# Weight splitting moves off GpSimd, and the bookkeeping of the choice moves to PSUM, in a gated attention and expert kernel

## The reference, cut to what matters

```
x = x + tanh(g_xattn) * mix(layernorm(x), softmax(q(ctx) k(ctx)^T))
n = layernorm(x)
logits = gelu(n @ rw1) @ rw2                 # 8 experts
wgt, idx = top_k(softmax(logits), 2)
for e in range(8):
    Ye = gelu(n @ w1[e] + b1[e]) @ w2[e] + b2[e]
    Ce = gelu(b1[e]) @ w2[e] + b2[e]
    for k in range(2):
        out += any(idx[..., k] == e) * wgt[..., k] * where(idx[..., k] == e, Ye, Ce)
x = x + tanh(g_ffn) * out
```

## Time and profile before

| | us |
|---|---|
| median of 3 runs | 200.49 |
| the 3 runs | 199.53 to 202.08 |
| the profiled execution | 201.76 |
| its span | 199.9 |
| busy, PE / DVE / ACT / POOL | 161.8 / 133.5 / 102.4 / 115.6 |
| mean granted TensorE clock | 0.939 of full speed |

### The profile page before, as it was taken

How to read it: one execution, slowest core, us unless ns; L and a number is a source line. 1 busy time by engine, 2 the same in 40 slices (tenths; PEclk the granted TensorE clock), 3 DMA queues, 4 the chain that set the end, 5 groups by cost and what they waited for, 6 DMA issues and landing times.

```text
span 199.9 us, 5212 instructions
## 1 busy us (share of the span) xinstructions
PE 161.8 (81%) x1722; PEld 137.8 (69%) x1723; DVE 133.5 (67%) x294; ACT 102.4 (51%) x256; POOL 115.6 (58%) x173
## 2 busy tenths in 40 slices
PE   6899995948169999599498599699499999998930
PEld 2457983814059999499397599598499999886610
DVE  2666589788635779989996266945566677464185
ACT  0588977727828999469487144243044433440000
POOL 0029999999868999678886414454155444203100
PEclk9999999996967999889999999999999999999955
DMA  6899354598377655945509435556166666430495
GB/s 178 252 387 331 123 152 169 181 279 271 118 211 256 232 175 201 320 147 177 197 21 387 139 113 225 216 228 234 46 241 249 247 232 219 192 113 33 125 325 200
DMA packets 21028, 40.69 MB, mean 204 GB/s; under 512 B 2741, under 2 KB 12047, under 8 KB 21010
## 3 DMA queue, kind: packets, MB, share of 16 engines
q1 hardware_dynamic: 17680, 34.54, 49.6%
q0 software_dynamic: 1872, 4.73, 7.4%
q10 hardware_dynamic: 1458, 1.19, 1.8%
HBM read 23.66 MB, written 4.60 MB: 141 GB/s over the span
## 4 chain that ended last, share of the span: by engine, by line
PE 45%; POOL 17%; DVE 13%; DMA 11%; issue 7%; SPq 3%; DVEq 1%; ACT 1%; POOLq 0%; ACTq 0%
POOL w_lo L401 11%; PE bank L1299 8%; PE bank L1301 7%; PE bank L1300 7%; PE bank L1310 7%; PE bank L1312 7%; PE bank L1311 7%; DMA stage<-in_L_ffn_w 4%; POOL w_hi L408 3%; DMA stage<-y_table 3%; DVE lnT L952 2%; DMA x_table<-probT 2%; DMA probT<-x_table,gidx 2%; DVE en L923 2%; DMA y_table<-lnx,ycol 1%
## 5 line engine op out<-in xcount | busy, mean ns | idle before, releaser
L654 ACT ACTIVATE bank<-bank,b1T 128x128 f32<-128x128 f32 x152 | 42.3, 342 | 57.7 <-PE bank L1301 57.7
L1310 PE MATMUL bank<-w_hi,cf 128*128 (+1 forms) x152 | 41.8, 275 | 9.8 <-DVE lnT L952 9.8
L401 POOL TENSOR_TENSOR w_lo<-stage,w_hi 128x256 bf16<-128x256 f32 x64 | 48.2, 787 | 0.7
L1311 PE MATMUL bank<-w_lo,cf 128*128 (+1 forms) x152 | 41.8, 275 | 0.8 <-issue 0.8
L1312 PE MATMUL bank<-w_hi,lnT 128*128 (+1 forms) x152 | 41.9, 276 | 0.0
L1300 PE MATMUL bank<-cfT,stage 128*128 128x128 bf16 x176 | 34.0, 219 | 0.0
L1299 PE MATMUL bank<-cfT,stage 128*128 128x128 f16 x176 | 34.0, 219 | 0.0
L1301 PE MATMUL bank<-cfT,stage 128*128 128x128 f16 x176 | 34.0, 219 | 0.0
L418 POOL TENSOR_TENSOR held<-cst 128x1 f32<-128x1 f32 x31 | 6.8, 218 | 39.0 <-DVE lnx L965 37.7
L952 DVE TENSOR_TENSOR lnT<-bank,cf 128x512 bf16<-128x512 f32 x38 | 26.1, 688 | 4.0 <-ACT cf L661 3.3
L519 ACT ACTIVATE w_hi<-stage 128x1024 f16<-128x1024 f32 x24 | 25.0, 1049 | 7.1 <-POOL cfT L414 5.6
(11 more groups left out here) (195 smaller groups left out, 340.7 us busy)
## 6 DMA issues: line engine op xcount, KB each, us to landing
stage<-in_L_ffn_w SPq DMA_DIRECT2D x32, 512.0 KB, 4.6
stage<-w_hi SPq DMA_DIRECT2D x12, 512.0 KB, 3.0
stage<-w_lo SPq DMA_DIRECT2D x12, 512.0 KB, 3.7
stage<-y_table SPq DMA_DIRECT2D x8, 256.0 KB, 4.7
xs<-in_x SPq DMA_DIRECT2D x2, 512.0 KB, 7.9
out<-stage SPq DMA_DIRECT2D x4, 256.0 KB, 2.7
cf<-in_ctx SPq DMA_DIRECT2D x1, 512.0 KB, 5.4
x_table<-cfT ACTq DMA_DIRECT2D x2, 256.0 KB, 4.2
```

What stands on the lines that cost most here:

```text
L401: last = nc.gpsimd.tensor_tensor(out=w_lo[:, q, n:n + PIECE], in0=stage[:, q % RING, n:n + PIECE], in1=w_hi[:, q, n:n + PIECE], op=ALU.sub ...
L654: last = nc.scalar.activation(h, h, ACT.Gelu, bias=bias)
L1310: mm(o, h_hi[:, u, c, :], w2_hi[:, ex, 1, c, :], start=(c == 0), stop=False)
L1311: mm(o, h_hi[:, u, c, :], w2_lo[:, ex, 1, c, :], start=False, stop=False)
```

## The change

- ScalarE and VectorE take over quarters that GpSimd split: `POOL_HIGHS` loses 9 and 27, `DVE_QUARTERS` becomes 6, 7 and all from 11 on. GpSimd keeps 0 to 5 whole and the low parts of 8, 9 and 10. Behind the index it issues DMAs only.
- GpSimd does the four `token_low` before the low parts 8 to 10; ScalarE does its `token_high` and `xnT_copy(1)` earlier, and its highs 8 to 11 among the sends.
- ScalarE does highs 12 to 15 ahead of block 0, and 16 to 31 in the 16 halves of the static blocks, one behind each.
- VectorE has new lists `ahead` and `behind`; the bookkeeping steps stand in front of `behind` and write their scratch to PSUM (`aside`, halves of banks 2 and 3, and bank 5) where it was SBUF.
- SyncE waits for the first gather before quarter 16, where it was 17.
- TensorE's register loads move from behind block 7 into it, and there are more `keep_busy` products: 4 and 4 new in the router stage, 12 for 6, 8 for 4, 14 for 9.

```diff
-        DVE_QUARTERS = (6, 7, 11, 12, 13, 15, 17, 19, 20, 22, 23, 26, 28, 29, 30, 31)
-        POOL_HIGHS = (0, 1, 2, 3, 4, 5, 9, 27)
+        DVE_QUARTERS = (6, 7) + tuple(range(11, QUARTERS))
+        POOL_HIGHS = (0, 1, 2, 3, 4, 5)
...
-                if q == 17:
+                if q == 16:
                     sp.wait_ge(gathered[0], 16)
...
             own(0, 6)
-            lows(8, 9)
-            token_low(0)
-            own(9, 10)
-            token_low(1)
-            token_low(2)
-            token_low(3)
-            lows(10, 11)
+            for b in range(4):
+                token_low(b)
+            lows(8, 11)
             wait(index_ready, 1)
...
-            lows(14, 15)
             refill(6, 0, 2, 16)
-            lows(16, 17)
             wait(yidx_ready, 1)
             put(0, 0)
             refill(7, 1, 3, 16)
-            lows(18, 19)
-            put(1, 1)
-            lows(21, 22)
-            put(2, 0)
-            lows(24, 25)
+            for i in range(1, 4):
+                put(i, i % 2)
...
-            high(13, 17)
+            high(12, 16)
...
+            later = [q for q in range(16, QUARTERS) if q not in POOL_HIGHS]
             for i in range(NS):
                 for half in range(2):
                     gelu_half(i, i % 2, i, half)
                     hidden_high(i, i % 2, half)
-                    q = 17 + 2 * i + half
-                    if q >= 27:
-                        q += 1
-                    high(q, min(q + 1, QUARTERS))
+                    if 2 * i + half < len(later):
+                        high(later[2 * i + half], later[2 * i + half] + 1)
...
-                step(nc.vector.tensor_tensor(out=en[:, :], in0=en[:, :], in1=eend, op=ALU.add))
...
-                step(nc.vector.tensor_tensor(out=oh_rest, in0=iota_b[:, N_EXP:BLOCKS].unsqueeze(1).broadcast_to(kb),
+                step(nc.vector.tensor_tensor(out=same, in0=iota_b[:, N_EXP:BLOCKS].unsqueeze(1).broadcast_to(kb),
                                              in1=blk_i.unsqueeze(2).broadcast_to(kb), op=ALU.is_equal))
...
-            low(11)
-            low(12)
-            scatter_rows(0, N_EXP)
+            scatter_rows(0, N_EXP, first, scratch[:, 0:N_EXP])
             counts_of_choices()
             dve.wait_ge(tr_w, 2)
             nc.vector.tensor_copy(b1T[:, :], bank[7][:, 0:HC * N_EXP])
+            low(11)
             xT_copy(0, 0)
+            low(12)
+            xT_copy(1, 1)
             low(13)
-            xT_copy(1, 1)
             hidden_low(0, 0, 0)
-            ahead = {0: (15,), 1: (19,), 2: (20,), 3: (22,), 4: (23,), 5: (26,), 6: (30,)}
-            behind = {0: (17,), 5: (28, 29), 6: (31,)}
+            ahead = {0: (14, 15), 1: (17,), 2: (19, 20), 3: (22,), 4: (24, 25), 5: (27, 28), 6: (30,)}
+            behind = {0: (16,), 1: (18,), 2: (21,), 3: (23,), 4: (26,), 5: (29,), 6: (31,)}
...
             xnT_tr(1)
+            keep_busy(4, 1, filler)
             router_hidden(1)
+            keep_busy(4, 1, filler)
...
+                        if i == NS - 1 and c == 1:
+                            pe.wait_ge(eb_ready, 1)
+                            pe.reg_mov(experts[0], NS - 1)
+                            pe.load(experts[1], eb[0:1, 2 * JS:2 * JS + 1])
+                        elif i == NS - 1 and c == 3:
+                            pe.wait_ge(used_ready, 1)
+                            jl = last_pair(pe)
+                        elif i == NS - 1 and c == 5:
+                            used = used_blocks(pe)
...
-            pe.wait_ge(eb_ready, 1)
-            pe.reg_mov(experts[0], NS - 1)
-            pe.load(experts[1], eb[0:1, 2 * JS:2 * JS + 1])
-            pe.wait_ge(used_ready, 1)
-            jl, used = last_pair(pe), used_blocks(pe)
             wait_weights(pe, QUARTERS - 1)
```

More of the change, by code:

```diff
@@ L474, in _ @@
             refill(7, 1, 3, 16)
-            lows(18, 19)
-            put(1, 1)
-            lows(21, 22)
-            put(2, 0)
-            lows(24, 25)
+            for i in range(1, 4):
+                put(i, i % 2)
             wait(index_ready, 2)
             refill(NS, 0, 4, 32)
-            put(3, 1)
-            lows(25, 26)
-            own(27, 28)
             put(4, 0)
@@ L903, in rest_of_blocks @@
+            def rest_of_blocks(spare):
+                starts = spare[:, 0:N_EXP]
+                rslot, blk_i = [spare[:, TOPK * T * n:TOPK * T * (n + 1)].bitcast(I32) for n in (1, 2)]
+                slotb = spare[:, TE:2 * TE].rearrange("p (t e) -> p t e", t=T)
+                rprod = spare[:, 2 * TE:4 * TE].rearrange("p (k t e) -> p k t e", k=TOPK, t=T)
+                same = bank[5][:, D:D + TOPK * T * REST].rearrange("p (k n) -> p k n", n=REST)
                 rank_te = rank_s[:, :].rearrange("p (t e) -> p t e", t=T)
-                step(nc.vector.tensor_tensor(out=slotb, in0=rank_te, in1=e_bc(st_[:, :]), op=ALU.add))
+                step(nc.vector.tensor_copy(starts, st_[:, :]))
+                step(nc.vector.tensor_tensor(out=slotb, in0=rank_te, in1=e_bc(starts), op=ALU.add))
@@ L917, in rest_of_blocks, with experts_of_blocks @@
                                         in1=tokp1.rearrange("p k t -> p (k t)").unsqueeze(2).broadcast_to(kb),
                                         op=ALU.mult).then_inc(rest_ready, 1)
-            def experts_of_blocks():
-                step(nc.vector.scalar_tensor_tensor(out=en[:, :], in0=more[:, 0:N_EXP], scalar=float(P), in1=st_[:, :],
-                                                    op0=ALU.mult, op1=ALU.add))
-                step(nc.vector.tensor_tensor(out=en[:, :], in0=en[:, :], in1=eend, op=ALU.add))
+            def experts_of_blocks(spare):
+                ends = spare[:, 0:N_EXP]
+                found = spare[:, 2 * N_EXP:2 * N_EXP + BLOCKS]
@@ new lines, in experts_of_blocks @@
+                step(nc.vector.tensor_copy(ends, en[:, :]))
+                step(nc.vector.scalar_tensor_tensor(out=behind_end, in0=iota_b.unsqueeze(2).broadcast_to(be),
+                                                    scalar=float(P), in1=ends.unsqueeze(1).broadcast_to(be),
+                                                    op0=ALU.subtract, op1=ALU.is_ge))
+                step(nc.vector.tensor_reduce(out=found, in_=behind_end, axis=X, op=ALU.add))
+                nc.vector.tensor_scalar(eb[:, :], found, float(N_EXP - 1), None, ALU.min).then_inc(eb_ready, 1)
@@ new lines, in used_counts @@
+            def used_counts(spare):
+                ends = spare[:, 0:N_EXP]
+                used_f = spare[:, N_EXP:N_EXP + 3]
+                whole = spare[:, 2 * N_EXP:2 * N_EXP + 3].bitcast(I32)
+                used = ((0, P + LEAST_LAST * 2 * P, 2 * P), (1, LEAST_ODD * 2 * P, 2 * P), (2, LEAST * P, P))
+                for n, least, size in used:
+                    last = nc.vector.tensor_scalar(used_f[:, n:n + 1], ends[:, N_EXP - 1:N_EXP], float(least - P), None,
+                                                   ALU.subtract)
+                step(last)
+                step(nc.vector.tensor_copy(whole, used_f))
+                for n, least, size in used:
+                    last = nc.vector.tensor_scalar(used_i[:, n:n + 1], whole[:, n:n + 1], size.bit_length() - 1, None,
+                                                   ALU.logical_shift_right)
+                last.then_inc(used_ready, 1)
```

106 lines of the change are left out of this document (43 added, 63 removed).

## The result

| | us |
|---|---|
| before, median of 4 runs | 200.92 (199.53 to 202.08) |
| after, median of 4 runs | **215.18** (213.03 to 216.37) |
| ratio, 95% interval | 1.0677 (1.0543 to 1.0811) |
| after, profiled execution / its span | 213.03 / 210.9 |
| mean granted clock, before / after | 0.939 / 0.935 |

The change is slower by 6.8%, and the forecast of 213.5 holds. The two profiled executions, 201.76 and 213.03, lie 11.3 us apart. All that follows compares spans and places within the profiled executions.

A forecast was written before the change was run, and what follows sets the result against it. GpSimd bounds the kernel ahead of block 0, TensorE from there on. Terms -2.0 - 0.8 - 9.7 + 0.7 + 4.2 + 16.3 + 4.5 = +13.2 on 201.76 give 215.0, stated as a 213.5 us median, range 206 to 219.

The forecast's parts named there:

- start and fillers: Ahead of and in block 0: earlier first gather, -2.0 us, and more dummy products raising block 0's clock, -0.8 us.
- waits of the blocks 1 to 4 that go: TensorE's waits of 2.2 and 2.9 us behind VectorE's stalled steps, and 1.45 us of low clock, disappear: -6.6 us.
- VectorE's excess: VectorE's loop turns 1 to 4 outlast TensorE's 5.5 us, giving waits of about one us at blocks 3 to 6: +4.2.
- four chains of late highs, with their clock: Blocks 6 to 8: TensorE waits on engines taking turns, +16.3 us, and the clock falls between, +4.5 us.
- loads in block 7: TensorE's register loads leave the end of block 7, saving 3.1 us, and cost 0.7 (0 to 3.1) between its columns.
- The late highs: Highs 28 to 31 stand behind gelus of blocks 6 and 7; four chains of 4.84 us, waits of 4.2: +16.3 us.
- "faster" rival: The highs are ready at each VectorE low, so the chain and its clock drop out: 192.9 us, chance 0.05.
- The clock: Blocks 6 to 8: three falls of 1.5 us behind the four idle stretches, +4.5 us (0 to +7.5).
- The start: Ahead of block 0: first gather at 49.6 instead of 52.63 us, 1.0 given back beside VectorE's low(11): -2.0 us.
- A rule on GpSimd's DMAs: First gather: the skill's 3100 ns for a DMA of 620 would put it, and the sum, 1.5 us later.
- What goes: Blocks 2 to 8: PSUM scratch frees two stalled steps, one low clock goes, loads leave block 7's end: -9.7 us.
- The fillers: Dummy products in the router stage, around the choice and ahead of block 0 shorten idle time: -0.8 us (0 to -1.5).

The follow-up runs named there:

- experiment 1: Changed kernel with ScalarE's high parts early again (22 and 23 together, 25 and 26 together), so 28 to 31 stand behind blocks 5 and 6: 195.06 us, ratio 0.9725.
- experiment 2: Kernel before with only the highs of quarters 28 to 31 one block later, behind the gelus of blocks 6 and 7: 214.65 us, ratio 1.0735.
- experiment 9: Changed kernel with the low parts of quarters 16, 21 and 26 back on GpSimd, ScalarE's high parts still late: 213.73 us, ratio 1.0774.
- experiment 4: Kernel before with only TensorE's register loads moved into block 7 (columns 1, 3 and 5): 199.88 us, ratio 1.0003.
- experiment 3: Kernel before with only the bookkeeping functions of the change, scratch of the choice steps in PSUM: 195.75 us, ratio 0.9789.
- experiment 7: Kernel of experiment 1 with the low parts of quarters 16, 21 and 26 given back to GpSimd: 192.48 us, ratio 0.9591.
- experiment 5: Kernel before with only the change's added dummy products (12, 8 and 14, and 4 behind each router transpose): 201.19 us, ratio 0.9965.
- experiment 8: Kernel of experiment 1 with the dummy products as before (6, 4 and 9, none behind the router transposes): 193.35 us, ratio 0.9619.
- experiment 10: Kernel of experiment 7 with the dummy products as before (6, 4, 9 and none behind the router transposes): 193.66 us, ratio 0.9639.
- experiment 11: Kernel of experiment 1 with TensorE's register loads put back behind block 7: 197.71 us, ratio 0.9895.
- experiment 6: Kernel before with only GpSimd's order changed, its four low parts of the tokens ahead of quarters 8 to 10: 201.74 us.
- experiment 12: Kernel before with the change's order ahead of the index on both GpSimd and ScalarE, quarter 9's high part on ScalarE: 199.4 us, ratio 0.9972.

## Why the prediction was right, step by step

The working was against the profiled execution, where it said +13.2 and the two profiled executions show +11.3. (215.0 less 1.27 is 213.7; the forecast said 213.5.) By its own terms, from the `y_copy` times above:

| | forecast | in the trace |
|---|---|---|
| start and fillers | -2.8 | -4.9 |
| waits of the blocks 1 to 4 that go, VectorE's excess | -6.6 + 4.2 = -2.4 | -2.8 |
| four chains of late highs, with their clock | +16.3 + 4.5 = +20.8 | +22 |
| loads in block 7 | -3.1 + 0.7 = -2.4 | -3.1 |

The loads' -3.1 is the 3.09 us that before loses there, and the +22 is what then remains of the 18.8 us between the `y_copy` of blocks 4 and 7. Some of the nearness of the total is chance: the start came out 2.1 us better than forecast and the clock 1.8 worse, which nearly cancels.

- **The late highs** are the step that decided the sign, and it held in its place, its order and its size. The forecast had waits of 4.2 us from a chain of 4.84; measured were 4.07, 3.42, 4.07 and 3.96, and the chain from the first gelu at 92.95 to the product at 97.64 is 4.69, where the forecast, without its first link of 0.19, has 4.65. Block 6 ends 20.0 us later than by before's pace, and of the low clock 1.9 us lie behind that, which makes 22. Experiments 1 and 2 show the cause by taking it out and by putting it in alone (-20.1 and +13.7 us). That it isn't VectorE's load is shown by experiment 2, which has VectorE's old list, and by experiment 9, which takes three low parts from it. The forecast's "faster" rival needed high 28 to be ready when VectorE came to its low part; VectorE waited 2.26 to 6.58 us each time.
- **The clock** was put too low: 6.3 us, where three falls of 1.5 were taken, 4.5 in all. All four pieces ran mostly at the low level, as the upper end of the term (7.5) had it. The pure waits were then a little less than forecast: about 22 - 6.3 = 15.7 against 16.3.
- **The start** was underrated by 2.1 us, if the two profiled executions are taken as they are. But the one of before has a late block 0: in experiments 2 and 4, which have before's start unchanged, `y_copy` of block 0 is at 67.08 and 66.73 instead of 68.64. So 1.6 to 1.9 of the 4.9 can be the execution and not the change, and 3.0 to 3.3 are then left against the forecast's 2.8. GpSimd's working came out nearly to the number: low parts of the tokens done at 41.15 (forecast 41.6), the gather at 48.89 (49.6). What did not come was the microsecond given back for `low(11)` beside the first gather: that gather took 1.12 us with `low(11)` beginning 0.27 us behind it, as long as before, and its data landed after 2.91 us instead of 3.60. TensorE began at 51.85 (forecast 54). One reading of the forecast was wrong: in the chain of before GpSimd's splitting doesn't run without a break up to the first gather. From 45.64 on the chain goes over ScalarE's queue, two high parts and the last transfer of the tokens to the table:

```profile
47.87 3.88 DMA x_table<-probT
```

It landed at 51.75, and GpSimd's last four pieces ended at 52.31. In experiment 3, where those pieces took 3.53 us instead of 4.52, GpSimd waited 1.25 us for the same transfer. So two things came late together in the kernel before, and the four `token_low` at the front of the list move both.
- **A rule on GpSimd's DMAs.** The forecast weighed the 3100 ns against 620 that the Trainium skill, page "SBUF — State Buffer", section "SBUF: two separate sides", gives for a DMA whose descriptors GpSimd can't write beside VectorE. The page gives them for a `tensor_copy` on VectorE; a `low` is a `tensor_tensor`, which by its subsection "Who interferes with whom" did not stall a DMA in the probe described there. So the page spoke less against the change than the forecast had it. The traces lie between the two. Gathers that begin while a `low` is already running are longer than the undisturbed 0.95: 1.83 us at 52.84 beside a `low` from 52.63 to 53.85, and in experiment 1 1.65 at 50.44 beside one up to 51.26, 1.92 at 56.37 beside one up to 57.46, and 1.14 at 53.66 beside one up to 53.98. The lengthening, 0.88, 0.70, 0.97 and 0.19, is each time a little less than what was left of the `low` (1.01, 0.82, 1.09 and 0.32). The first gather, which began ahead of the `low`, paid nothing.
- **What goes.** The two steps that stood still go with the PSUM scratch (experiment 3), and that alone gives 2.1%, 4 to 5 us; the fall of the clock at 83 to 86 us goes with them. The Trainium skill, page "SBUF — State Buffer", section "Who interferes with whom", says that a VectorE instruction with two inputs in SBUF contends with a GpSimd instruction that reads SBUF, and that the port is locked for one of them alone. With one input moved to PSUM the 2.18 us became 0.43 in experiment 3 while GpSimd was splitting, and the trace agrees.
- **VectorE's excess** came as forecast, as waits of about one us: 0.69, 1.10, 1.20 and 0.52 at 73, 77, 87 and 91 us, 3.5 in all for 4.2. In the same stretch experiment 1 waits 4.2 us and experiment 7, with three low parts less on VectorE, 1.9.
- **The loads** cost nothing inside block 7 (5.53 us from transposes to transposes in experiment 4), the lower end of what was allowed (0 to +3.1).
- **The fillers** gave nothing that can be measured (experiments 5 and 8), where -0.8 was taken. In the trace of after the clock was low in block 0 all the same (0.50 from 54 to 56 us).

What stays open: on what it depends whether the clock falls behind a wait of 2.8 us or not. At the same place of the program, in or behind the same wait of 2.8 us, it fell in the traces of experiments 1, 4, 7, 8, 10 and 11, and not in those of before, after and experiments 2, 3, 5, 6, 9 and 12. Each is one execution, so it isn't shown either whether this belongs to the kernel or to the execution. No run here was made to settle that. Nor was the move of the low parts from GpSimd to VectorE tried alone; experiment 7 takes back three of them.

## What to carry to other kernels

When work moves between engines, write down for each consumer the order in which its inputs come out of the producer's list, and look for an item that stands behind something that needs the consumer's own progress: four items one block too late cost 20 us here, although every engine had idle time. An item's cost is not its 1 us of work but the whole round through the engines that then take turns. Parts of a change are to be tried apart: this one holds a part that gives 2% (scratch in PSUM), one that costs 7% (the place of four high parts) and some that show nothing measurable alone. With that one place mended it is 3% faster than the kernel before (195.06), and with three low parts given back to GpSimd besides, 4% (192.48).

## What the runs showed of the hardware

- The same wait is followed by full clock in one trace and by the 1.2 GHz level in another: 2.85 us, then 1.00 (before) or 0.68 (experiment 4), and so in eight and six traces of the fourteen here. So a microsecond or two gained ahead can be lost again by the clock behind.
- A gather of GpSimd that begins during a step of VectorE with two inputs in SBUF is lengthened by 0.2 to 1.0 us, in the four cases read above by a little less than what is left of the step, and not where it begins ahead of it (1.12).
- It works in the other direction as well: four pieces of GpSimd's splitting take 2.55 us with no `low` beside them (experiment 7), and 3.71 and 5.40 beside VectorE's lows (experiments 7 and 3).
